# Cross-attention with a quantised FFN: the value product takes x scaled but not centred, and the mean comes off where x1 leaves PSUM

## The reference

```python
def _layernorm(x, eps=1e-05):
    m = mean(x, -1); v = var(x, -1)
    return (x - m) / sqrt(v + eps)

# cross-attention: query and key both come from the context
q = ctx @ Wq.T + bq;  k = ctx @ Wk.T + bk            # 512 x 128
attention = softmax(q @ k.T, axis=-1)                # 512 x 512, every row sums to 1
x1 = x + layernorm(x) @ attention.T                  # the value product
# feed-forward with MXINT8 quantisation of activations and weights in blocks of 32
v = layernorm(x1)                                    # rounded to bf16 further on
h = bf16(layernorm_w(v));  h = bf16(quant(h) @ quant(W1).T + b1)
h = bf16(gelu(h));         h = bf16(quant(h) @ quant(W2).T + b2)
out = x1 + bf16(v + h)
```

## Time and profile before

| | |
|---|---|
| median of three runs | 283.07 us (282.75 to 284.05) |
| profiled execution, its own time | 283.25 us |
| its span, first to last instruction | 281.4 us |
| busy DVE | 249.2 us, 89% of the span, 377 instructions |
| busy PE | 228.7 us, 81% |
| busy ACT | 169.4 us, 60% |
| busy POOL | 69.0 us, 25% |
| chain that ended last, by engine | DVE 45%, PE 25%, ACT 11%, DMA 8%, issue 5%, POOL 4% |
| mean granted clock of PE | 0.927 of full speed |

### The profile page before, as it was taken

One profiled execution on the slowest core, in us unless ns is written; L12 is line 12 of the kernel. 1 busy time (PEld: TensorE's weight loads), 2 busy tenths in 40 slices (PEclk: granted clock), 3 DMA queues, 4 the chain that ended last, 5 costly groups with the idle time before them and its releaser, 6 DMA issues.

```text
span 281.4 us, 3244 instructions
## 1 busy us (share of the span) xinstructions
PE 228.7 (81%) x937; PEld 99.4 (35%) x946; DVE 249.2 (89%) x377; ACT 169.4 (60%) x287; POOL 69.0 (25%) x96
## 2 busy tenths in 40 slices
PE   7748739996998059651699969799999989999993
PEld 7314313443433024210244433344444434444431
DVE  2388999999988899999979999599999999877992
ACT  2337216628995447845987599966566554665610
POOL 1058100022004500053060050413333233333400
PEclk9985886999999759975899999999999999999999
DMA  4963999999997952939623045635355555555683
GB/s 157 378 250 89 227 279 201 297 238 194 263 257 190 221 91 38 222 59 194 124 52 62 0 93 70 119 62 123 88 122 129 130 130 131 130 130 114 139 178 130
DMA packets 103077, 42.92 MB, mean 152 GB/s; under 512 B 93844, under 2 KB 96152, under 8 KB 102552
## 3 DMA queue, kind: packets, MB, share of 16 engines
q1 hardware_dynamic: 100224, 35.93, 58.6%
q10 hardware_dynamic: 2360, 6.83, 7.7%
q0 software_dynamic: 480, 0.02, 0.1%
HBM read 15.48 MB, written 4.19 MB: 70 GB/s over the span
## 4 chain that ended last, share of the span: by engine, by line
DVE 45%; PE 25%; ACT 11%; DMA 8%; issue 5%; POOL 4%; SPq 2%; ACTq 0%; DVEq 0%; POOLq 0%
DVE amax L764 12%; PE ps L722 9%; PE ps L712 8%; PE ps L661 4%; DVE w_int L807 4%; DMA xhl<-pf 3%; DVE hq L966 3%; DVE stats L918 3%; DMA wst<-in_L_ffn_W 3%; DVE vw L961 3%; DVE pf L871 3%; DVE phl L942 2%; DVE wquant L861 2%; POOL rs L350 2%; DVE xhl L954 2%
## 5 line engine op out<-in xcount | busy, mean ns | idle before, releaser
L661 PE MATMUL ps<-pT,xT 128*128 128x512 f16 x192 | 49.7, 414 | 14.1 <-DMA pT<-phl 11.0
L722 PE MATMUL ps<-w2T,xhl 128*128 128x512 bf16 x247 | 56.5, 379 | 2.9 <-DMA xhl<-pf 2.4
L712 PE MATMUL ps<-w1T,cxT 128*128 128x512 bf16 x256 | 58.0, 380 | 0.0
L558 ACT ACTIVATE wst<-ps 128x1024 bf16<-128x1024 f32 x32 | 32.3, 1019 | 27.9 <-PE ps L712 27.9
L764 DVE TENSOR_REDUCE amax<-phl 128x64 f32<-128x2048 bf16 x16 | 36.5, 2280 | 6.9 <-ACT phl L562 6.9
L649 PE MATMUL ps<-qkT 128*128 128x512 f32 x32 | 19.5, 715 | 22.7 <-ACT pf L457 18.8
L661 PEld LDWEIGHTS ps<-pT,xT 128*128 128x128 f16 x192 | 19.9, 106 | 48.0 <-issue 31.8
L722 PEld LDWEIGHTS ps<-w2T,xhl 128*128 128x128 bf16 x256 | 24.6, 98 | 33.2 <-DMA xhl<-pf 4.2
L712 PEld LDWEIGHTS ps<-w1T,cxT 128*128 128x128 bf16 x256 | 23.7, 98 | 32.6 <-issue 6.2
L562 ACT ACTIVATE phl<-wst 128x2048 bf16<-128x2048 bf16 x16 | 30.6, 1910 | 1.3
L423 POOL TENSOR_TENSOR wst<-wst,vs 128x512 bf16<-128x512 bf16 x12 | 14.8, 1233 | 55.5 <-DVE wquant L866 55.5
(11 more groups left out here) (79 smaller groups left out, 357.4 us busy)
## 6 DMA issues: line engine op xcount, KB each, us to landing
wst<-in_L_ffn_W ACTq DMA_DIRECT2D x6, 1024.0 KB, 6.1
xs<-in_x SPq DMA_DIRECT2D x4, 1024.0 KB, 8.4
out_x<-wst SPq DMA_DIRECT2D x16, 256.0 KB, 2.8
cx<-in_ctx SPq DMA_DIRECT2D x4, 512.0 KB, 5.8
wst<-in_L_ffn_W SPq DMA_DIRECT2D x2, 1024.0 KB, 10.3
xhl<-pf SPq DMA_TRANSPOSE x17, 4.3
xT<-xhl SPq DMA_TRANSPOSE x16, 4.6
pT<-phl SPq DMA_TRANSPOSE x16, 3.3
```

Of the source, the lines that this page charges most:

```text
L558: act.activation(ys[:, k, 1024 * g:1024 * g + 1024], ps_y[:, 2 * g:2 * g + 2, :], ACT.Copy)\
L661: pe.matmul(ps_pv[:, t % 2, :], xT[:, t, NT * a + n, :], pT[:, :, NT * c + n, :], start=(s == 0), stop=False)
L712: last = pe.matmul(ps_y[:, c, :], h1T[:, k, t, :], w1T[:, 4 * c:4 * c + 4, t, :], start=False, stop=(t == KT - 1))
L722: last = pe.matmul(ps_z[:, k, :], h2T[:, k, t, :], w2T[:, t, :], start=False, stop=(t == FT - 1))
```

## The change

`normalise` goes. `x_high` now reads `xs` itself and multiplies by `rs` while it rounds to float16; `x_low` becomes a SCALAR_TENSOR_TENSOR that multiplies `xs` by `rs` again and subtracts the high part, as `p_low` does for p. XSCALE falls from 2^10 to 2^3 and is folded into `rs` (the variance is multiplied by XSCALE^-2 before the power -0.5). POOL gets one more small operation per batch: instead of `rx` it computes `mscaled` = -mean/XSCALE and `mr` = mscaled times rs, that is -mean times 1/sqrt(v + eps). `x_plus` adds `mr` as a per-row bias, so its function is Identity in place of Copy. `x_high` waits for POOL's `rs` alone, not for DVE.

```diff
-XSCALE = 2.0 ** 10
+XSCALE = 2.0 ** 3
...
             def factors_x(b):
                 wait_alone(pool, mvr, LT * (b + 1), pool_gate)
-                wait_alone(pool, xn_rdy, LT * b, pool_gate)
-                pool.tensor_scalar(rs[:, 0, :, 0], mv[:, :, 1], EPS, None, ALU.add).then_inc(ve[0], 1)
+                wait_alone(pool, x_lo, LT * b, pool_gate)
+                pool.tensor_scalar(rs[:, 0, :, 0], mv[:, :, 1], EPS, XSCALE ** -2, ALU.add, ALU.mult).then_inc(ve[0], 1)
                 rsqrt(0, b)
+                wait_alone(pool, mr_rdy, b, pool_gate)
+                pool.tensor_scalar(mscaled[:, :], mv[:, :, 0], -1.0 / XSCALE, None, ALU.mult).then_inc(ms_rdy, 1)
                 wait_alone(pool, rsr[0], b + 1, pool_gate)
-                pool.tensor_scalar(rx[:, :], rs[:, 0, :, 1], XSCALE, None, ALU.mult).then_inc(rx_rdy, 1)
+                wait_alone(pool, ms_rdy, b + 1, pool_gate)
+                pool.tensor_tensor(mr[:, b, :], mscaled[:, :], rs[:, 0, :, 1], ALU.mult).then_inc(mr_rdy, 1)
...
             def x_high(b, t):
-                act.wait_ge(xn_rdy, b * LT + (t + 1))
+                act.wait_ge(rsr[0], b + 1)
                 wait(act, xT_rdy[t], 16 * b)
-                act.activation(xhl[:, t, 0, :], xn[:, t % 2, :], ACT.Copy).then_inc(x_hi, 1)
+                act.activation(xhl[:, t, 0, :], xs[:, LT * b + t, :], ACT.Copy, scale=rs[:, 0, t, 1:2])\
+                   .then_inc(x_hi, 1)
...
             def x_plus(b, t):
 
+                if t == 0:
+                    wait_alone(act, mr_rdy, b + 1, act_gate)
                 wait_alone(act, pv_ps, b * LT + (t + 1), act_gate)
-                act.activation(xs[:, LT * b + t, :], ps_pv[:, t % 2, :], ACT.Copy,
+                act.activation(xs[:, LT * b + t, :], ps_pv[:, t % 2, :], ACT.Identity, bias=mr[:, b, t:t + 1],
                                scale=1.0 / (XSCALE * PSCALE), accum_out=sums[:, 0, 0, t:t + 1])\
...
-            def normalise(b, t):
-                if t == 0:
-                    dve.wait_ge(rx_rdy, b + 1)
-                wait_alone(dve, x_lo, b * LT + (t - 1), dve_gate)
-                dve.tensor_scalar(xn[:, t % 2, :], xs[:, LT * b + t, :], mv[:, t, 0:1], rx[:, t:t + 1],
-                                  ALU.subtract, ALU.mult).then_inc(xn_rdy, 1)
-
             def x_low(b, t):
                 dve.wait_ge(x_hi, b * LT + (t + 1))
-                dve.tensor_tensor(xhl[:, t, 1, :], xn[:, t % 2, :], xhl[:, t, 0, :], ALU.subtract)\
-                   .then_inc(x_lo, 1)
+                dve.scalar_tensor_tensor(xhl[:, t, 1, :], xs[:, LT * b + t, :], rs[:, 0, t, 1:2], xhl[:, t, 0, :],
+                                         ALU.mult, ALU.subtract).then_inc(x_lo, 1)
...
                 negmax(b, 3)
-                normalise(b, 3)
                 recip(b, 2)
```

More of the change, by code:

```diff
@@ L81, in xattn_ffn_kernel @@
         qkT = sb("qkT", [P, 2, N], F32)
-        xn = sb("xn", [P, 2, H], F32)
         vw = sb("vw", [P, 2, H], F32)
@@ L97, in xattn_ffn_kernel @@
         rs = sb("rs", [P, 3, LT, 2], F32)
-        rx = sb("rx", [P, LT], F32)
+        mr = sb("mr", [P, B, LT], F32)
+        mscaled = sb("mscaled", [P, LT], F32)
         off = sb("off", [P, LT], F32)
@@ L154, in xattn_ffn_kernel @@
         wT_ps, cT_ps, qk_ps, e_ps, pv_ps = (sem(n) for n in ("wT_ps", "cT_ps", "qk_ps", "e_ps", "pv_ps"))
-        wT_sb, cT_sb, qk_sb, p_exp, p_hi, xn_rdy, x_hi = (
-            sem(n) for n in ("wT_sb", "cT_sb", "qk_sb", "p_exp", "p_hi", "xn_rdy", "x_hi"))
+        wT_sb, cT_sb, qk_sb, p_exp, p_hi, x_hi = (
+            sem(n) for n in ("wT_sb", "cT_sb", "qk_sb", "p_exp", "p_hi", "x_hi"))
         x1_rdy, x1_sq, v_rdy, v_sum, v_sq = (sem(n) for n in ("x1_rdy", "x1_sq", "v_rdy", "v_sum", "v_sq"))
@@ L169, in xattn_ffn_kernel @@
         v_mean, v_mean2, v_ms = sem("v_mean"), sem("v_mean2"), sem("v_ms")
-        rx_rdy = sem("rx_rdy")
+        ms_rdy, mr_rdy = sem("ms_rdy"), sem("mr_rdy")
         xT_rdy = [sem(f"xT_rdy{t}") for t in range(LT)]
@@ L919, in x_stats @@
                 if isinstance(b, int) and b > 0:
-                    dve.wait_ge(rx_rdy, b)
+                    dve.wait_ge(ms_rdy, b)
                 for t in range(LT):
@@ L974, in front @@
                 negmax(b, 0)
-                normalise(b, 0)
                 if w1 is not None:
@@ L979, in front @@
                 negmax(b, 1)
-                normalise(b, 1)
                 recip(b, 0)
@@ L993, in front @@
                 negmax(b, 2)
-                normalise(b, 2)
                 recip(b, 1)
```

## The result

The changed kernel took **279.23 us** (median of 5 runs, 278.78 to 282.78), the kernel before 283.92 beside it (5 runs, 282.75 to 285.82). The two medians lie 4.7 us apart; the ratio with its 95% interval, 0.989 (0.985 to 0.994), says 3.0 us less (1.6 to 4.4), and I go by that. Two further measurements of the same pair gave 0.986 (0.981 to 0.991) and 0.989 (0.982 to 0.995).

A forecast was written before the change was run, and what follows sets the result against it. DVE was taken to bound the front's last window (busy 41.68 of 42.20 us), with waits elsewhere swallowing savings. -0.25 up to `times_w(0, 0)` and -1.58 in batch 3 sum to -1.83: 281.4 us; 8-in-10 range 279.3 to 283.6.

The forecast's parts named there:

- Prices: Per-instruction costs: 16 `xn` removed, 7.2 us; `x_low` +0.06, `x_high` +0.09, `x_plus` +0.1 each; DVE -6.2, ACT +3.0 us.
- Batch 3: From `times_w(0, 0)` to the end of `w_mult(W1, 3)`: all four `xn` count, -1.82, four `x_low` +0.24: -1.58 us.
- Batch 1: DVE's wait for PE's fourth energies swallows three of four `xn`; afterwards one `xn` -0.45 and two `x_low` +0.12.
- Batch 0: First `x_high` needs `rs` alone, -0.86; two `x_high` +0.18, one `x_low` +0.06: -0.6 us at the last pT transpose.
- The clock after that: At `values(0, 0)`: if PE's clock returns at the same moment, half of batch 0's 0.6 us is lost: 281.7.
- Batch 2: ACT's additions +0.37 leave -0.55 at `p_low(2, 2)`; POOL's `mr` +0.25 leaves DVE -0.25 at `times_w(0, 0)`.
- `mr`'s +0.25: POOL's extra operation costs 0.25 us ahead of `times_w(0, 0)`; bounds 0 and 1.2.
- the other reading of the prediction: `mr` costs nothing, because POOL's next operation was shut out by DVE's `p_low` before anyway; the sum 0.25 us lower.
- Up to the FFN: Transposes of h1 move with DVE's `w_mult`; the four last `x_plus` taken as nothing, at most +0.2 us.
- DVE as the bound everywhere: Rival: all 6.2 us of DVE count, 277.0 us; in whole or part 277.0 to 280.6, chance 0.17.
- `factors_v(1)` late: Rival: DVE waits for POOL before `times_w(1, 0)`, batch 3's -1.58 vanishes, 283.0 us; chance 0.24 with another rival.
- ACT as the bound: Rival: ACT's chain releases DVE in batches 2 and 3, adding 1.5 us: 284.8 us; chance 0.09.

The follow-up runs named there:

- spare3: Changed kernel with a spare DVE instruction of the removed pass's form, awaited by nobody, at its four places in batch 3 alone; 282.22 us, ratio 0.989.
- dep0: Changed kernel with batch 0's `x_high` waiting for DVE again, through spare instructions of the old pass's form; 281.82 us, ratio 0.994.
- spare_all: Changed kernel with the spare DVE instruction, awaited by nobody, at all sixteen places of the removed pass; 283.32 us, ratio 1.000.
- w2late: Kernel before the change with one edit: ACT issues W2's load behind the context copy and v work; 284.73 us, ratio 1.002.
- nomr: Changed kernel without POOL's multiplication for `mr`, so it computes something else; 281.07 us, ratio 0.992.
- again2: Changed kernel with no edit, measured and profiled a third time; median 280.55 us.
- again: Changed kernel with no edit, measured and profiled a second time; median 280.24 us.
- warm: Changed kernel with 44 dummy 128 x 128 matmuls on PE in four stretches where it waits, to keep its clock up; 280.20 us.

## Why the prediction was right

- **Prices: right.** `x_low` 745 ns against 742 forecast, `x_high` 712 against 712, `x_plus` 676 against 686. DVE 5.8 us less busy (6.2), ACT 2.3 more (3.0).
- **Batch 3: right.** -1.58 forecast, -1.61 in all three profiles, and spare3 takes it back with the same four steps. From `times_w(0, 0)` to h1's transpose are 43.17, 43.15 and 43.14 us, against 44.75. This is the term that carries the forecast.
- **Batch 1: right.** Three of the four `xn` vanish in the wait at the fourth row maximum (DVE's idle there 2.44, 0.68 and 2.99 us, where over 1 was forecast), one counts: -0.29 for -0.33.
- **Batch 0: the mis-sized step.** "So -0.6 when DVE releases the last pT transpose": it was -1.65. The -0.86 of the first `x_high` stands (19.48 to 18.44, of which 0.09 is an earlier start: -0.95). What was left out is that ACT in batch 0 waited for PE as well, 0.82 us at the copy of the context, since PE's clock had fallen at about 20 us. The energies come a microsecond sooner and PE's gaps are shorter; in six of eleven profiles with the short path the clock held, and there this wait is gone too. dep0 shows the path, spare_all the same path without the clock's part (-0.94). That `values(0, 0)` then moves by the same amount did not come out: nmax(0, 0) to values is 26.35 before and 26.69, 23.89 and 25.15 after.
- **The clock after that: right in sign.** "Half of these 0.6 us are lost." The twelve matmuls of `values(0, 0)` take 4.2 to 4.5 us where batch 0 is as before (before, w2late, dep0), and 4.7 to 5.3 in the profiles with the shorter batch 0 and neither fillers ahead of it nor a smaller load; values to nmax(1, 3) is 0.15 to 1.2 longer than before. The granted clock came back 3.0 to 3.6 us after `values(0, 0)` began in the former and 3.9 to 6.0 in the latter. "TensorE: Matmul & The Clock Gate" ("What's actually happening") of the Trainium skill calls the monitor's window free-running. These traces agree in that the return keeps no fixed distance from PE's start; why it comes later behind the shorter batch 0 they do not show.
- **Batch 2: two terms off.** +0.37 of ACT's additions was rightly priced but offset by a stall that went, -0.5 (w2late), which the sum did not have; `mr`'s +0.25 was 0 (nomr), the other reading of the prediction. The two stages together came to -0.15 + 0.07 against +0.37 + 0.31, 0.76 us better than forecast.
- **Up to the FFN: right.** tw(1) to b1 is 13.23 before and after. Not seen was that PE's clock can fall ahead of the first product, in either kernel.
- **The rivals.** DVE as the bound everywhere (277.0) fell: it waits at all three places. The time lies in the part of the range given to this rival (277.0 to 280.6), but by other ways than its own: nmax(2, 0) to exp(2, 1) is 3.97 as before, so ACT's stretch did not yield to an earlier start. `factors_v(1)` late (283.0) fell: `times_w(1, 0)` has no idle time ahead of it in any profile. ACT as the bound (284.8) fell: DVE had no wait for it in batch 3.
- **A sign that could not serve.** "If `times_w(0, 0)` moves by more than 1 us" the forecast was to be wrong. It moved by +0.46, -3.06 and -1.32 us in the three profiles, most of it in stretches that scatter by more than that. And two thirds of 0.50 with rival 1's 0.17 are 0.50, where the prediction has 0.52.

In sum, for again2 against before: 0.93 is the start, which lies ahead of the change; batches 0 to 2 give -1.65 + 0.45 + 1.19 - 0.29 - 0.01 - 0.15 + 0.07 = -0.39, batch 3 -1.61, the FFN -0.27, together 3.2 of span. In this profile all of batch 0's 1.65 was given back by batch 1's last row maximum; in again, whose transposes landed sooner (-0.80), almost nothing was (+0.15). Of the 3.0 us that the ratio says, 1.6 are batch 3, as forecast, and 0.4 the stages from nmax(1, 3) to tw(0), where the forecast had 0.35 of loss; the rest, some 1.0, would have to lie in batch 0 and the FFN, and within the interval (1.6 to 4.4) it could be nothing. How much is left of batch 0 on average the runs do not settle. That faster came out is the mechanism of batch 3; that the time came out so far below the forecast is in part terms that I had wrong.

## What to carry to other kernels

An instruction taken off an engine counts where that engine is alone at the limit, and there for its step (0.45 us) and not for its length (0.54); but if it stood between two other engines it shortens their path at once (by 0.9 us or more in batch 0), which counts only as far as a later wait doesn't take it back. Look for second waits on the same path: at each place where the shortened path meets another engine's wait (ACT for PE 0.82, ACT's own DMA issue 0.40), the forecast is short by that wait. And when a step is worth tenths while the kernel's medians scatter by 1 us, compare distances between marks of several profiles.

## What the hardware showed that I had not expected

- A DMA issue in ACT's list that waits for another engine held ACT's next instruction for 0.40 us, though ACT had work that did not need the data.
- The granted clock at 20 us stayed at 1.00 with gaps of 1.45 and 0.39 us ahead of PE's two pairs of energies and was 0.50 with gaps of 1.49 and 0.40 (spare_all), but 1.00 again in spare3 with 1.68 and 0.39: a kernel can sit on the edge, and one profile doesn't tell on which side.
- Fillers cost PE's time even at the upper level: the 40 of warm from 36.95 take 4.72 us at a granted clock of 0.98, and PE's real work stood behind them.
- One more 128 x 4 operation of POOL ahead of one that DVE's `p_low` already held up cost nothing (11.10 us from p_low(2, 2) to tw(0) with it and without).
